# Third attention of a fused transformer kernel: the norm of the experts' sum taken into the attention, the bias products moved, the lower rows added by gpsimd

## The reference, cut to what matters

```python
# second feed-forward: attention over the samples, then 8 experts with the two best per row
x1  = ln(z + attention(z)) * ln1_g + ln1_b
y   = x1 + share0 * expert_a(x1) + share1 * expert_b(x1)
x   = x + (ln(y) * ln2_g + ln2_b)
# third attention: 16 heads, 77 keys from the context, a relative position bias
h   = ln(x)
q, k, v = h @ Wq, ctx @ Wk, ctx @ Wv
p   = softmax(q @ k.T + bias[bucket(k_pos - q_pos)])
x   = x + (p @ v) @ Wo
```

## Time and profile before

| | us |
|---|---|
| runs (median, lowest, highest of 3) | 1353.63, 1350.27, 1355.65 |
| profiled execution: its own time | 1364.73 |
| profiled execution: span from first to last instruction | 1362.9 |
| mean granted TensorE clock in it | 0.901 of full |
| end of the last expert | 1016 |
| third attention from its first statistics to its last tile | 1061 to 1221 |
| TensorE busy over the span | 1128.2 (83%) |
| VectorE busy over the span | 765.7 (56%) |
| gpsimd busy over the span | 497.9 (37%) |

### The profile page before, as it was taken

The page is one execution under the profiler, slowest core; times in us unless marked ns, Lnnn a source line. Parts: engine busy times, 40 slices in busy tenths (PEclk is TensorE's granted clock), DMA queues, the critical chain, the costliest instruction groups (busy, mean ns, idle before and its releaser), DMA issues.

```text
span 1362.9 us, 20740 instructions
## 1 busy us (share of the span) xinstructions
PE 1128.2 (83%) x7405; PEld 945.7 (69%) x7405; DVE 765.7 (56%) x1719; ACT 418.9 (31%) x869; POOL 497.9 (37%) x453
## 2 busy tenths in 40 slices
PE   6889698886488969899956999998895599876896
PEld 4778576664377756698856999997784477764564
DVE  3667767665566644788851222221228577738584
ACT  2345432221256521111101222221122244440365
POOL 4434512244456511376755111004006244320243
PEclk9789899998699979799877999999897699997798
DMA  7999000000100020000035242112112000000001
GB/s 279 386 387 379 1 0 1 20 1 0 74 1 1 1 88 0 1 1 17 31 124 225 100 158 98 38 35 73 46 35 75 1 1 2 1 1 1 0 24 39
DMA packets 43732, 93.59 MB, mean 69 GB/s; under 512 B 3821, under 2 KB 17806, under 8 KB 40838
## 3 DMA queue, kind: packets, MB, share of 16 engines
q1 hardware_dynamic: 35254, 62.24, 12.7%
q0 software_dynamic: 7104, 29.14, 5.9%
q10 hardware_dynamic: 1296, 1.18, 0.2%
HBM read 39.02 MB, written 51.51 MB: 66 GB/s over the span
## 4 chain that ended last, share of the span: by engine, by line
PE 55%; issue 21%; DVE 14%; ACT 5%; POOL 2%; DMA 1%; another core or an unknown queue 1%; SPq 0%; POOLq 0%; DVEq 0%; ACTq 0%
PE PS L1949 10%; PE PS L1959 9%; PE PS L870 7%; PE PS L1217 3%; PE PS L883 3%; PE PS L853 3%; PE PS L843 3%; PE PS L825 2%; PE PS L738 2%; PE PS L822 1%; PE PS L877 1%; PE PS L1207 1%; PE PS L1244 1%; DVE scr L2090 1%
## 5 line engine op out<-in xcount | busy, mean ns | idle before, releaser
L1949 PEld LDWEIGHTS PS<-scr 128*128 128x128 f32 x992 | 121.1, 198 | 9.0 <-issue 6.0
L1949 PE MATMUL PS<-scr 128*128 128x128 f32 x992 | 123.3, 283 | 4.7 <-ACT scr L1977 3.1
L588 POOL TENSOR_TENSOR scr<-scr,big 128x1232 f32<-128x1232 f32 x32 | 72.0, 2249 | 131.3 <-DVE big L396 131.3
L1959 PE MATMUL PS<-scr 128*128 128x256 f32 x496 | 113.5, 381 | 6.9 <-issue 6.9
L1982 ACT ACTIVATE scr<-PS,W 128x128 f32<-128x128 f32 x148 | 53.6, 367 | 199.2 <-PE PS L1949 194.6
L2012 DVE TENSOR_SCALAR scr<-PS,W 128x128 f32<-128x128 f32 x148 | 51.4, 351 | 98.5 <-PE PS L1949 87.7
L1959 PEld LDWEIGHTS PS<-scr 128*128 128x128 f32 x496 | 91.8, 191 | 19.2 <-issue 8.1
L691 ACT ACTIVATE big<-PS 128x512 f32<-128x512 f32 x144 | 74.5, 525 | 92.0 <-PE PS L853 91.7
L853 PE MATMUL PS<-W,scr 128*128 128x128 f32 x480 | 81.7, 293 | 21.5 <-ACT scr L686 8.1
L870 PEld LDWEIGHTS PS<-scr,big 128*128 128x128 f32 x640 | 85.3, 200 | 7.3 <-issue 5.5
L870 PE MATMUL PS<-scr,big 128*128 128x34 f32 (+1 forms) x640 | 87.4, 279 | 0.0
(11 more groups left out here) (407 smaller groups left out, 2457.6 us busy)
## 6 DMA issues: line engine op xcount, KB each, us to landing
expert_in<-zeros SPq DMA_DIRECT2D x1, 19712.0 KB, 55.3
expert_out<-zeros SPq DMA_DIRECT2D x1, 19712.0 KB, 106.6
scr<-ew_in POOLq DMA_DIRECT2D x12, 1024.0 KB, 6.6
scr<-expert_in SPq DMA_DIRECT2D x38, 128.0 KB
big<-ew_in POOLq DMA_DIRECT2D x4, 1024.0 KB, 9.1
expert_out<-scr POOLq DMA_DIRECT2D x28, 128.0 KB, 2.0
W<-pack SPq DMA_DIRECT2D x1, 2458.0 KB, 8.6
W<-pack SPq DMA_DIRECT2D x1, 2152.0 KB, 8.3
```

Of the source, the lines that this page charges most:

```text
L588: g.tensor_tensor(sc3, sc3, a_mx[u % 3].unsqueeze(2).broadcast_to([P, H, S2]), ALU.subtract).then_inc(s["sub_ready"], 1)
L1949: ins = pe.matmul(bank(1 + f % 4, G), e_w1[slot][:, k, f * P:(f + 1) * P], e_xT[:, k, :], start=(k == 0), stop=(k == C - 1))
L1959: ins = pe.matmul(bank(5 + t, D), e_h[:, f, t * P:(t + 1) * P], e_w2[slot][:, f, :], start=(f == 0), stop=(f == FC - 1))
```

## The change

The stage norm2 is gone, its barrier with it. Its parts go to three places.

The norm of a sample becomes rows_summed (one pair of scalar_tensor_tensor, as the lower rows are in X1 already) and rows_added on VectorE, rows_rstd and upper_gathered on gpsimd, all inside the third attention: samples 0 to 3 before its loop, the sum of 4 to 7 in the odd iterations 1 to 7 after z_of, the addition of 3 to 7 in the even iterations 0 to 8 before stats_of.

The six bias products go to the end of samp: TensorE makes part n at the end of its iteration 16 + n, parts 4 and 5 behind the last, ScalarE copies them one iteration later, with a semaphore, bias_taken, for the two banks that are used twice.

gpsimd, done with the gathers of the lower rows in the last expert, waits for them and does lower_added: two halves, each a multiplication by the shares and an addition to X1, over 128x2048.

Besides, TensorE makes the four value products first and does both scores(0) and scores(1) before z and q of sample 1; some buffers move: y of the norm behind the values in scr, the attention's transposed probabilities, outputs and queries into the third quarter of big, the finished rows r_Z into the fourth, small vectors into small.

```diff
@@ -473,10 +477,22 @@
                 ch.link(v.tensor_reduce(a_par, blk.rearrange("p (j w) -> p w j", w=2), AX.X, ALU.add))
                 ch.inc(v.tensor_copy(a_mask.rearrange("p t (w s) -> p t w s", w=2),
                                      w["mask0"].rearrange("p (t s) -> p t s", t=T).unsqueeze(2).broadcast_to([P, T, 2, S2])))
-            stats_of(0)
-            z_of(0)
-            stats_of(1)
-            z_of(1)
+            if lay == 2:
+                rows_summed(v, ch, 0)
+                rows_summed(v, ch, 1)
+                rows_added(v, ch, 0)
+                stats_of(0)
+                rows_added(v, ch, 1)
+                z_of(0)
+                stats_of(1)
+                rows_summed(v, ch, 2)
+                z_of(1)
+                rows_added(v, ch, 2)
+            else:
+                stats_of(0)
+                z_of(0)
+                stats_of(1)
+                z_of(1)
             if lay == 0:
                 v.wait_ge(s["v_psum"], 5)
                 v.tensor_copy(a_bvT, bank(7, C).unsqueeze(2).broadcast_to([P, C, P])).then_inc(s["w_centered"], 1)
@@ -489,6 +505,8 @@
                 query_vars(1)
                 head_normed(0)
                 z_of(3)
+            if lay == 2:
+                rows_summed(v, ch, 3)
             scores(0)
             scores(1)
             if lay == 1:
@@ -519,7 +537,11 @@
                 if j < B:
                     if odd:
                         z_of(j)
+                        if lay == 2 and j + 1 < B:
+                            rows_summed(v, ch, j + 1)
                     else:
+                        if lay == 2:
+                            rows_added(v, ch, j)
                         stats_of(j)
                 if lay == 2 and u >= 2:
                     if not odd:
@@ -588,8 +610,22 @@
                 g.tensor_tensor(sc3, sc3, a_mx[u % 3].unsqueeze(2).broadcast_to([P, H, S2]),
                                 ALU.subtract).then_inc(s["sub_ready"], 1)
+            if lay == 2:
+                upper_gathered(g, 0)
+                upper_gathered(g, 1)
+                v_ones(g, 2)
+                rows_rstd(g, 0)
+                upper_gathered(g, 2)
+                rows_rstd(g, 1)
+                upper_gathered(g, 3)
             rstd_of(0)
+            if lay == 2:
+                upper_gathered(g, 4)
             rstd_of(1)
+            if lay == 2:
+                upper_gathered(g, 5)
+                rows_rstd(g, 2)
+                upper_gathered(g, 6)
             if lay == 0:
                 g.wait_ge(s["v_kept"], 4)
                 for c, k, r0, r1, h, s0, s1 in PIECES[1::2]:
@@ -600,6 +636,9 @@
                 rstd_of(3)
                 query_rstd(1)
             else:
+                if lay == 2:
+                    upper_gathered(g, 7)
+                    rows_rstd(g, 3)
                 subtracted(0)
                 subtracted(1)
             if lay != 2:
@@ -617,6 +656,8 @@
                     biased(i + 1)
                 if not odd and i + AHEAD[lay] + 1 < B:
                     rstd_of(i + AHEAD[lay] + 1)
+                if lay == 2 and odd and i + 4 < B:
+                    rows_rstd(g, i + 4)
                 if lay == 2 and odd and i >= 1:
                     row_based(i - 1)
                 if lay == 2 and not odd and i >= 1:
@@ -895,6 +936,9 @@
             if lay == 0:
                 pe.wait_ge(s["v_kept"], 4)
                 out_biases()
+            if lay == 2:
+                scores(0)
+                scores(1)
             extra("z", 1)
             extra("q", 1)
             if lay == 0:
@@ -902,8 +946,9 @@
             if lay == 1:
                 for kind, j in (("kt", 0), ("qt", 0), ("z", 2), ("q", 2)):
                     extra(kind, j)
-            scores(0)
-            scores(1)
+            if lay != 2:
+                scores(0)
+                scores(1)
             if lay == 1:
                 extra("kt", 1)
                 extra("qt", 1)
@@ -1527,6 +1573,8 @@
         V_PSUM = PS[:, 0:4, :].rearrange("p b (r h d) -> p (b r) h d", r=2, h=H)
         LG_AT, RANK_AT, TOTAL_AT = D, D + UNITS * E, D + UNITS * E + 4 * E
         BIAS_PARTS = [(t, k0, min(32, S2 - k0)) for t in range(T) for k0 in range(0, S2, 32)]
+        BIAS_BANKS = (0, 1, 2, 3, 2, 3)
+        bias_taken = sem("bias_taken")
         rel4 = zeros[:, 0:4 * H]
         def bias_tables_sp(sp):
@@ -1543,6 +1591,8 @@
         def bias_products(pe, n, b):
             t, k0, kn = BIAS_PARTS[n]
+            if n >= 4:
+                pe.wait_ge(bias_taken, n - 1)
             for k in range(k0, k0 + kn, 4):
                 at = t * P + (S2 - 1) - k
                 kg = min(4, k0 + kn - k)
@@ -1553,7 +1603,8 @@
         def bias_kept(a, n, b):
             t, k0, kn = BIAS_PARTS[n]
             a.wait_ge(at_["w_centered"], 5 + n + 1)
-            return a.activation(BIAS2[:, t, :, k0:k0 + kn], bank(b, kn * H).rearrange("p (k h) -> p h k", h=H), ACT.Copy)
+            a.activation(BIAS2[:, t, :, k0:k0 + kn], bank(b, kn * H).rearrange("p (k h) -> p h k", h=H),
+                         ACT.Copy).then_inc(bias_taken, 1)
         def samp_dve(v, ch):
             s = samp
@@ -1806,6 +1857,10 @@
                     n = BATCHES[q][1] - BATCHES[q][0]
                     a.wait_ge(s["top_ready"], q + 1)
                     a.activation(x_dif[:, 0:n, :], x_dif[:, 0:n, :], ACT.Exp).then_inc(s["texp_ready"], 1)
+                if it > UNITS:
+                    bias_kept(a, it - UNITS - 1, BIAS_BANKS[it - UNITS - 1])
+            for n in range(LAST - UNITS, len(BIAS_PARTS)):
+                bias_kept(a, n, BIAS_BANKS[n])
         def samp_pe(pe):
             s = samp
@@ -1888,6 +1943,12 @@
                     values_summed(it)
                 if it + 2 in ON_PE:
                     products_summed(it + 2)
+                if it == UNITS:
+                    pe.wait_ge(rows_zeroed, 16 * 9)
+                if it >= UNITS:
+                    bias_products(pe, it - UNITS, BIAS_BANKS[it - UNITS])
+            for n in range(LAST + 1 - UNITS, len(BIAS_PARTS)):
+                bias_products(pe, n, BIAS_BANKS[n])
             pe.sem_inc(moe["xT_psum"], 1)
@@ -2060,6 +2121,19 @@
                     weights_load(g, e + 3, e % 3)
             for i in range(B):
                 gathered(g, i, 0, rows_moved)
+            g.wait_ge(rows_moved, 16 * 3 * NT)
+            for half in range(2):
+                lower_added(g, half)
+        def lower_added(g, half):
+            b = slice(half * B // 2, (half + 1) * B // 2)
+            samples = lambda m: m.rearrange("p (b t) d -> p b t d", t=T)[:, b, :, :]
+            rows, x1 = samples(got(0)), samples(m_X1)
+            share = PART[:, 0, :].rearrange("p (t b) -> p b t", t=T)[:, b, :].unsqueeze(3).broadcast_to([P, B // 2, T, D])
+            g.tensor_tensor(rows, rows, share, ALU.mult).then_inc(pool_chain, 1)
+            pool_steps[0] += 1
+            g.wait_ge(pool_chain, pool_steps[0])
+            g.tensor_tensor(x1, x1, rows, ALU.add)
         ARRIVALS = [(0,), (1,), (2, 3), (4, 5), (6,), (7,)]
@@ -2075,66 +2149,43 @@
...
+        def rows_summed(v, ch, i):
+            y = n_y[i % 2]
+            v.wait_ge(rows_gathered[arrival_of(i)], 16 * T * len(ARRIVALS[arrival_of(i)]))
+            for t in range(T):
+                n = T * i + t
+                ch.inc(v.scalar_tensor_tensor(out=y[:, t, :], in0=got(1)[:, n, :], scalar=PART[:, 1, unit_of(n):unit_of(n) + 1],
+                                              in1=m_X1[:, n, :], op0=ALU.mult, op1=ALU.add))
+            ch.sync()
+            for t in range(T):
+                ch.inc(v.bn_stats(n_stats[i % 2][:, t, :], y[:, t, :]))
+            ch.sync()
+            for t in range(T):
+                ins = v.bn_aggr(n_mv[i % 2][:, t, :], n_stats[i % 2][:, t, :])
+            ins.then_inc(var_ready, 1)
+        def rows_added(v, ch, i):
+            y = n_y[i % 2]
+            v.wait_ge(rstd_ready, nth(norm2, i) + 1)
+            for t in range(T):
+                ch.inc(v.scalar_tensor_tensor(out=y[:, t, :], in0=y[:, t, :], scalar=n_mv[i % 2][:, t, 0:1], in1=w["ln2g"],
+                                              op0=ALU.subtract, op1=ALU.mult))
+            ch.sync()
+            for t in range(T):
+                xt = X[:, T * i + t, :]
+                ins = v.scalar_tensor_tensor(out=xt, in0=y[:, t, :], scalar=n_rstd[i % 2][:, t:t + 1], in1=xt,
+                                             op0=ALU.mult, op1=ALU.add)
+            ins.then_inc(z_ready, T)
+            v.wait_ge(z_ready, T * nth(norm2, i) + T)
+        def rows_rstd(g, i):
+            g.wait_ge(var_ready, nth(norm2, i) + 1)
+            power(g, n_rstd[i % 2], n_ve[i % 2], n_mv[i % 2][:, :, 1]).then_inc(rstd_ready, 1)
+        def upper_gathered(g, i):
+            gathered(g, i, 1, rows_gathered[arrival_of(i)])
         def last_sent(eng):
@@ -2142,10 +2193,12 @@
             eng.wait_ge(last_stored, 16 * stores + 16)
```

(26 more changed lines are left out.)

105 lines of the change are left out of this document (26 added, 79 removed).

## The result

The kernel after took 1367.09 us in the median of 4 runs (1364.76 to 1368.07), beside 1352.33 for the kernel before: a ratio of 1.0104, 95% interval 1.0061 to 1.0147. The change costs some 15 us. A second timing of the same kernel, beside other runs of the kernel before, gave 1.0138 (1.0099 to 1.0178).

A forecast was written before the change was run, and what follows sets the result against it. The prediction took VectorE's work to bound the stretch before the third attention's loop and, behind the residual, to lie on the loop's path. Terms -25.4 + 23.3 + 15.7 = +13.6 on 1353.6 gave 1367 us, range 1342 to 1376.

The forecast's parts named there:

- Part 1: Stretch before the third attention's loop: first probabilities at 1057.6 instead of 1083.05, a gain of 25.4 us.
- the six steps listed behind 1049.0: Before the loop: scores(1) 1.0, transposes 1.1, copy 0.65, product 3.75, copy 0.65, exps(0) 1.23, used as 8.6 us.
- The estimate of 2.2 us: Before the loop: three z_of of 0.74 starving gpsimd's descriptor writing would add 2.2 us to part 1.
- Part 2: Third attention's loop: VectorE's added work, with rows_added held by gpsimd's subtraction on even tiles, costs 23.3 us.
- Part 3: TensorE's clock in the loop: gaps of about 4 us put five odd tiles at the low level, costing 15.7 us.
- the 9.9 of the earlier trace: Kernel before: after 2.79 us of idling before the transposes, TensorE's clock stayed at 0.50 for 9.9 us.
- Part 4: Bias products in the sampling stage and lower rows in the last expert: both hidden, cost 0.
- the cover: End of the sampling stage: 4.5 us between the last batch's slots and the first scatter needing them; 2 us if it fails.
- The forecast of 13.6: Whole kernel: the sum of the parts, -25.4 + 23.3 + 15.7 = +13.6 us.
- Clock holds: Rival for the loop: port waits as forecast but the clock returns at once; -2, 1352 us, no change; chance 0.17.
- Port free: Rival for the loop: scalar_tensor_tensor isn't held; 1342 us at full clock (chance 0.18), 1350 with clock falls (0.08).
- Clock stays low through the first nine tiles: Rival for the loop: even tiles are at the low clock too, +22 in place of 15.7; 1374 us; chance 0.11.

The follow-up runs named there:

- the filler: The kernel after plus 16 matmuls that nobody reads, before TensorE's transposes in iterations 3, 5, 7 and 9: 1350.65 us, ratio 0.9995.
- the filler run: Under the rivals, the same run as the filler; under the hardware surprises (gap of 2.08 us), the kernel with the filler before the loop.
- the first experiment: The kernel after with rows_added of the even tiles moved into VectorE's gap before its scores: 1341.01 us, ratio 0.9939.
- the second experiment: The kernel after with both rows_added and rows_summed moved into VectorE's gap before its scores: 1327.05 us, ratio 0.983.
- the kernel with the filler before the loop: The kernel after with rows_added and rows_summed in VectorE's gap, z and q of sample 1 before both scores, 18 unread matmuls: 1327.75 us, ratio 0.9845.

## Why the prediction was right

The sum was 1367, the range 1342 to 1376, the chance of slower 0.57; measured 1367.09. Its steps, one by one.

**Part 1, -25.4.** -25.2 in the traces. Its two halves held: 28.7 us from the first gather to scores(0) (28.55 measured), and 10.1 from there to the probabilities (10.35). In the second half the six steps listed behind 1049.0 add up to 8.4 and not to the 8.6 that were used; measured, it is 8.9 from scores(1) at 1033.69 to the probabilities. That the order of TensorE takes 3.7 us back is shown by the two runs with the order undone. The estimate of 2.2 us by the Trainium skill's "SBUF — State Buffer", section "SBUF: two separate sides", for gpsimd's descriptors starved by z_of, didn't show in that size: the three gathers that began beside z_of took 1.01, 1.14 and 1.01 us where the shortest took 0.95, some 0.3 us in all; the longest, 1.29, ran beside rows_added.

**Part 2, +23.3.** The mechanism is shown twice, by moving the instruction out of the subtraction (0.88) and by moving it 0.97 us towards its end (1.52). Wherever it met one of these gpsimd operations its held instruction ended 0.27 to 0.29 us behind that one, whether it had taken 2.47 (tile 0), 2.19, 1.48 (beside L601) or 1.12; the forecast had 2.2 to 2.3 for the 2.19. Its wait in the loop is 2.59 - 0.87 = 1.72 (1.83 forecast), and the even tiles 2 to 8 take 10.67 us, +3.50 (3.63 forecast). Tile 0 came out at +3.9 for 4.0, but the low level has a part in it: in this trace TensorE, at the low level since 1028, stands only 0.97 us before the first L918, as it is late itself; in the second trace of the same kernel, which begins the loop at full clock, the gap is 4.07 and the stretch 10.2 us, +2.4. The Trainium skill's "SBUF — State Buffer", section "Who interferes with whom", has the VectorE instruction with two SBUF inputs contend with a gpsimd instruction that reads SBUF, and one with at most one SBUF input, outside the two-port modes, not. The traces agree: 1.52 to 2.59 against 0.85 to 0.88 for L2173, and 0.75 for bn_stats beside the subtraction. The 2.38 of L373, which has a single tensor input, is the exception that the sentence leaves room for; that L373 ran in a two-port mode no row shows.

**Part 3, +15.7.** The falls are where they were put in four of the five odd tiles, behind gaps of 3.86 to 4.34, and the filler shows them to be the cause of the length. The first odd tile was at the low level for another reason in this trace: TensorE had not left it since 1028; in the second trace the clock fell there too behind a gap, of 4.07. The size was too small. The odd tiles took 12.8, 13.0, 15.1, 14.2 and 15.4 us, 70.5 in all, where 65.3 were forecast, since behind L918 the low level lasts 11 to 12 us in four of them, nearly to the end of L866 or past it (3.38 to 3.76 instead of 1.97), and not the 9.9 of the earlier trace rows; only the fourth has some 9.8. The odd tiles' whole addition is 26.0 instead of 20.5; the even ones' 14.0 instead of 14.5. So the loop was forecast 5 us too short.

**Part 4, 0.** Each edit alone in the kernel before: nothing for the bias products, whose last slots came 1.8 us later, within the 2 that were allowed and under the cover; the lower rows hidden in the last expert (their four operations take 16.3 us, 18 forecast, done by 975.6) and a gain of 5 in the norm.

**The sum against the median.** By the two traces the third attention lost 18.7 us (3.9 + 40.0 - 25.2), by the medians the kernel lost 14.8 and, on the second occasion, 19.5. One trace is a thin base: in the three runs that leave the loop as it was (the two edits of part 4, and the norm ahead of the loop) the stretch from turned(0) to turned(9) takes 77.3 to 77.4 us instead of 73.2 and the one before it 10.5 instead of 7.8, as the first tiles run at the low level. With the bias products moved and all else as before, the first sum to turned(9) is 147.9 us, against 141.0 in the trace of before and 157.7 and 159.7 in the two of after: a loss of 10 to 19 us, by which traces are compared, and against a loop of 77.3 us the kernel after's 113.2 are 36 more, 1 us over the forecast and not 5. The forecast of 13.6 lies inside; that it met the median within 0.1 us is luck, and one of its terms was 5 us short by the trace that it was worked out from.

**The rivals.** "Clock holds" is what the filler run made: -2 was forecast, ratio 0.9995 measured. "Port free" is close to what the first experiment made by moving the instruction. "Clock stays low through the first nine tiles" is out: the even tiles have 1.00.

## What to carry to other kernels

Work that is put into a tuned loop is priced by its place in the engine's order and hardly by its length: the same VectorE work cost 40 us behind the residual and 5 in the gap where VectorE waits for TensorE anyway (36 and 1 against the loops of 77.3 us), 1367 against 1327 us. Before you choose the place, look for the engine's own idle slot in one iteration, ask what gpsimd runs at that moment, and what gap the busiest engine is left with and whether its clock survives it. When a change promises a shorter lead-in, price the loop it lengthens with its multiplicity first.

## What was not expected of the hardware

The low level can outlast nearly unbroken work. In the second odd tile TensorE was busy for 11.74 of 11.80 us at 0.51, and then had 1.00 in the following tile. The fall itself can come late: in the filler run the gap of 2.08 us ended at 1035.12, and the clock was still 1.00 up to 1036.60.

The length of a single gap is no safe guide to the clock. Of the gaps before TensorE's L918 in the third attention, over all fourteen traces, every one of 1.50 us and more that began at full clock has a fall beside it, before its end or within 2 us behind it; 1.50, 1.64, 1.73 and 1.76 are among them, and the earlier trace rows has 1.70 without a fall in the first feed-forward. Of the eight between 1.01 and 1.19 two have one (1.02 in the second experiment, 1.01 in the kernel with the filler before the loop), six have none, and neither has the 0.89 of the filled gap.

The last expert has a stall of 13 to 15 us in some executions, beside 16 gathers that run without it in others. Its cause wasn't looked for; the timed medians of the kernel before on the three occasions, 1350.51, 1361.45 and 1347.99, differ by nearly as much, and the highest is from the group whose traces all have it.
